# Six table chunks parted on ScalarE and TensorE, and one one-hot instruction for three pairs

## What is computed

```
emb = flat[ids + offs]
mask = (jnp.arange(L_) < lengths[..., None]).astype(emb.dtype)
pooled = jnp.einsum('bfle,bfl->bfe', emb, mask)
out = pooled.reshape(Bq, F_ * E_)
return jnp.nan_to_num(out)
```

## Time and profile before

| | |
|---|---|
| median of 3 runs | 1639.28 us |
| the profiled execution's own time | 1622.87 us |
| its span, first to last instruction | 1621.1 us |
| TensorE matmul, busy | 1003.0 us (62%) |
| VectorE, busy | 1065.0 us (66%) |
| ScalarE, busy | 509.2 us (31%) |
| GpSimd, busy | 760.1 us (47%) |
| mean granted TensorE clock | 0.792 of 2.4 GHz |
| DMA | 121.48 MB, mean 75 GB/s |

### The profile page before, as it was taken

One profiled execution on the slowest core, in us unless ns is written; L12 is line 12 of the kernel. 1 busy time (PEld: TensorE's weight loads), 2 busy tenths in 40 slices (PEclk: granted clock), 3 DMA queues, 4 the chain that ended last, 5 costly groups with the idle time before them and its releaser, 6 DMA issues.

```text
span 1621.1 us, 25785 instructions
## 1 busy us (share of the span) xinstructions
PE 1003.0 (62%) x8607; PEld 801.0 (49%) x8607; DVE 1065.0 (66%) x3021; ACT 509.2 (31%) x793; POOL 760.1 (47%) x706
## 2 busy tenths in 40 slices
PE   2757107692754816757588582881847538487886
PEld 0536006571643715636377360760735437276776
DVE  9938006793673916947599481891857629489894
ACT  2423004350422403324244140430423214143441
POOL 4845770537064172253666527166073442556110
PEclk9979558896786957968789685895877759689899
DMA  4312112132312213132334141231314113233120
GB/s 142 137 51 56 24 25 81 53 120 61 99 55 60 91 42 103 46 92 69 82 103 129 38 120 41 85 88 37 114 43 123 52 41 98 52 111 110 31 83 11
DMA packets 69225, 121.48 MB, mean 75 GB/s; under 512 B 33985, under 2 KB 35750, under 8 KB 69152
## 3 DMA queue, kind: packets, MB, share of 16 engines
q1 hardware_dynamic: 45936, 99.21, 19.0%
q0 software_dynamic: 22016, 20.93, 7.2%
q10 hardware_dynamic: 1200, 0.67, 0.2%
HBM read 79.67 MB, written 4.80 MB: 52 GB/s over the span
## 4 chain that ended last, share of the span: by engine, by line
DVE 44%; another core or an unknown queue 29%; PE 14%; issue 7%; DMA 2%; ACT 2%; SPq 1%; DVEq 0%; POOL 0%; POOLq 0%
DVE onehot_j L627 16%; PE sums L454 9%; DVE onehot_p L625 6%; DVE table L641 6%; DVE table L649 6%; DVE gathered L689 5%; PE pairs L444 4%; DMA table<-tables 2%; ACT counts L422 2%; DVE is_nan L659 1%; SPq L305 1%; DVE pooled L669 1%; DVE pooled L662 0%; DVEq L687 0%
## 5 line engine op out<-in xcount | busy, mean ns | idle before, releaser
L454 PE MATMUL sums<-table,counts 128*128 128x192 bf16 x7056 | 835.5, 262 | 209.3 <-issue 202.1
L422 ACT ACTIVATE counts<-pairs 128x588 int16<-128x588 f32 (+1 forms) x792 | 507.9, 653 | 1082.1 <-remote 547.1
L454 PEld LDWEIGHTS sums<-table,counts 128*128 128x128 fp8e3 x7056 | 667.0, 102 | 312.8 <-issue 258.3
L379 POOL DMA_INDIRECT rows<-tables,row_now x576 | 618.5, 1074 | 414.6 <-issue 414.6
L444 PE MATMUL pairs<-onehot_j,onehot_p 128*128 128x294 bf16 x1548 | 383.8, 315 | 390.2 <-ACT counts L422 164.4
L625 DVE TENSOR_TENSOR onehot_p<-ramp,p_of 128x256 bf16<-128x256 f16 x756 | 213.7, 283 | 435.1 <-remote 385.0
L627 DVE TENSOR_SCALAR onehot_j<-ramp,j_of,worth 128x296 bf16<-128x296 f16 x1512 | 493.6, 358 | 0.0
L444 PEld LDWEIGHTS pairs<-onehot_j,onehot_p 128*128 128x128 bf16 x1548 | 151.4, 101 | 488.5 <-issue 264.5
L389 POOL DMA_INDIRECT out_gathered<-gathered,place_now x56 | 70.2, 1254 | 394.0 <-DVE gathered L662 381.2
L641 DVE TENSOR_TENSOR table<-table 128x448 f32<-128x448 f32 (+1 forms) x180 | 144.4, 802 | 27.7 <-DMA table<-tables 27.0
L649 DVE TENSOR_TENSOR table<-table 128x448 f32<-128x448 f32 (+1 forms) x180 | 144.7, 804 | 0.0
(11 more groups left out here) (53 smaller groups left out, 49.0 us busy)
## 6 DMA issues: line engine op xcount, KB each, us to landing
table<-tables SPq DMA_DIRECT2D x126, 448.0 KB
rows<-zeros SPq DMA_DIRECT2D x56, 640.0 KB
rows<-tables,row_now POOLq DMA_INDIRECT x576
out_counted<-pooled SPq DMA_DIRECT2D x108, 21.0 KB
sorted_records<-records,rank POOLq DMA_INDIRECT x56
row_now<-sorted_records SPq DMA_DIRECT2D x56, 10.5 KB
out_gathered<-gathered,place_now POOLq DMA_INDIRECT x56
rows<-lookup_ids SPq DMA_DIRECT2D x1, 731.0 KB, 7.8
```

Of the source, the lines that this page charges most:

```text
L379: nc.gpsimd.indirect_dma_start(out=rows[:, k, l * E:(l + 1) * E], out_offset=None, in_=table_rows, in_offset=bass.IndirectOffsetOnAxis(ap= ...
L422: nc.scalar.activation(dst, src, ACT.Copy).then_inc(counts_saved, 1)
L454: last = nc.tensor.matmul(sums[h][:, k * PARTS * E:(k + 1) * PARTS * E], counts[h][:, j, :, k], parts[:, :, j, :, 1], start=(j == 0 and k ...
```

## The change

**Parting a chunk.** Chunks 0 to 5 of each table are no longer cut by VectorE. A new PSUM buffer `rest` of two banks holds one chunk, 448 numbers in each bank. ScalarE copies the fp32 chunk into it (`copy_chunk`). TensorE multiplies the first bf16 part by `minus_eye`, a matrix with -1 on the diagonal, and adds it onto `rest` (`take_away`, two matmuls of 448 columns), which leaves value minus first part. ScalarE writes that as bf16 into the place of the second part (`save_middle`), TensorE takes that away too, and ScalarE writes the third part (`save_low`). `PARTED_AT` gives the slot of a feature (0 to 41) at which each chunk begins: 9, 13, 17, 21, 25, 29. The three ScalarE instructions stand behind the `save_counts` of that slot and the next two; the two `take_away` stand behind the products of the next slot and the one after. A new chunk's copy waits until `rest` is read (`low_saved`). Chunk 6 stays with VectorE, in stage 12 as before.

**PSUM.** The two banks come from `pairs`, which has two buffers instead of three (`SETS = 2`).

**One-hots of p.** The three `onehot_p` instructions of a chunk become one of 128x768, ahead of the chunk's first `onehot_j`. It waits until the last pair of the chunk two stages earlier has been used.

**Start.** VectorE makes `minus_eye` once, and TensorE writes all 512 columns of both banks of `rest` once (`begin_rest`).

```diff
-SETS = 3
+SETS = 2
...
-CUTS = {3: (0, 0, 1), 4: (1, 0, 1), 5: (2, 0, 2), 6: (2, 1, 2), 7: (3, 0, 2), 8: (3, 1, 2), 9: (4, 0, 1),
-        10: (5, 0, 2), 11: (5, 1, 2), 12: (6, 0, 1)}
+PARTED_AT = {0: 9, 1: 13, 2: 17, 3: 21, 4: 25, 5: 29}
+
+PARTED_BY_VECTOR = {12: 6}
...
+        rest = psum("rest", [P, 2, 512], F32)
...
+            def copy_chunk(f, c):
+                if f == 0 and c == min(PARTED_AT):
+                    act.wait_ge(rest_begun, 1)
+                elif parted(f, c) > 1:
+                    act.wait_ge(low_saved, parted(f, c) - 1)
+                act.wait_ge(table_in[c], f * 16 + 16)
+                nc.scalar.activation(rest[:, :, 0:CE // 2], both_halves(0, c), ACT.Copy).then_inc(chunk_copied, 1)
+
+            def save_middle(f, c):
+                act.wait_ge(rest_ready, parted(f, c))
+                nc.scalar.activation(upper_of_both(1, c), rest[:, :, 0:CE // 2], ACT.Copy).then_inc(middle_ready, 1)
+
+            def save_low(f, c):
+                act.wait_ge(low_ready, parted(f, c))
+                nc.scalar.activation(upper_of_both(2, c), rest[:, :, 0:CE // 2], ACT.Copy).then_inc(low_saved, 1)
...
+                            u = slot(h, c, q)
+                            if u - 2 in begun_in:
+                                save_low(f, begun_in[u - 2])
+                            if u - 1 in begun_in:
+                                save_middle(f, begun_in[u - 1])
+                            if u in begun_in:
+                                copy_chunk(f, begun_in[u])
...
+            def begin_rest():
+
+                pe.wait_ge(eye_ready, 1)
+                pe.wait_ge(ramps_in, 32)
+                for x in range(2):
+                    last = nc.tensor.matmul(rest[:, x, :], minus_eye[:], ramp[:, 0:512], start=True, stop=True)
+                last.then_inc(rest_begun, 1)
+
+            def take_away(part, c, done):
+                for x, half in enumerate(halves_of(c)):
+                    last = nc.tensor.matmul(rest[:, x, 0:CE // 2], minus_eye[:], upper_halves(part)[:, half],
+                                            start=False, stop=True, skip_group_check=True)
+                last.then_inc(done, 1)
+
+            def part_table(f, u):
+
+                if u - 2 in begun_in:
+                    pe.wait_ge(middle_ready, parted(f, begun_in[u - 2]))
+                    take_away(1, begun_in[u - 2], low_ready)
+                if u - 1 in begun_in:
+                    pe.wait_ge(chunk_copied, parted(f, begun_in[u - 1]))
+                    take_away(0, begun_in[u - 1], rest_ready)
...
+                                if c in PARTED_AT:
+                                    pe.wait_ge(low_saved, parted(f, c))
+                                else:
+                                    pe.wait_ge(parts_ready, f * (CHUNKS - PARTED) + by_vector.index(c) + 1)
                                 pe.sem_inc(products_begun, 1)
                             multiply(1 - h, c * JC + q * JC // PAIRS, c * JC + (q + 1) * JC // PAIRS)
+                        if with_counts:
+                            part_table(f, slot(h, c, q))
...
+            def negate_eye():
+                dve.wait_ge(ramps_in, 32)
+                nc.vector.tensor_scalar(minus_eye[:], ramp_twice[:, :, 0], lane[:], -1.0, ALU.is_equal,
+                                        ALU.mult).then_inc(eye_ready, 1)
...
-                if i % 2 == 0:
+                if i == 0:
                     stage = f * STAGES + h * CHUNKS + c
                     if stage >= AHEAD:
-                        dve.wait_ge(counted, eviction_at(stage - AHEAD, i // 2) + 1)
-                    g = lookup_group(c, i)
-                    nc.vector.tensor_tensor(onehot_p[:, s, 1 + i // 2, :, :], ramp_twice,
-                                            p_of[:, 2 * f + h, g:g + 2].unsqueeze(1).to_broadcast([P, P, 2]), ALU.is_equal)
+                        dve.wait_ge(counted, eviction_at(stage - AHEAD, PAIRS - 1) + 1)
+                    of_chunk = p_of[:, 2 * f + h, c * PER_CHUNK:(c + 1) * PER_CHUNK].rearrange("p (k x) -> p k x", x=2)
+                    nc.vector.tensor_tensor(onehot_p[:, s, 1:, :, :], ramp_twice.unsqueeze(1).to_broadcast([P, PAIRS, P, 2]),
+                                            of_chunk.unsqueeze(2).to_broadcast([P, PAIRS, P, 2]), ALU.is_equal)
...
-            def cut_rest(f, c, part, parts):
-
-                sl = slice(c * CE + part * CE // parts, c * CE + (part + 1) * CE // parts)
-                if part == 0:
-
-                    dve.wait_ge(table_in[c], f * 16 + 16)
+            def cut_rest(f, c):
+
+                sl = slice(c * CE, (c + 1) * CE)
+                dve.wait_ge(table_in[c], f * 16 + 16)
...
-                    if stage in CUTS and i == 1:
-                        cut_rest(f, *CUTS[stage])
-                    if stage in CUTS and i == 4:
-                        cut_low(f, *CUTS[stage])
+                    if stage in PARTED_BY_VECTOR and i == 1:
+                        cut_rest(f, PARTED_BY_VECTOR[stage])
+                    if stage in PARTED_BY_VECTOR and i == 4:
+                        cut_low(f, PARTED_BY_VECTOR[stage])
```

40 lines of the change are left out of this document (30 added, 10 removed).

## The result

The changed kernel takes 1814.76 us (median of 4 runs, 1813.99 to 1818.2) against 1639.22 (4 runs, 1623.92 to 1640.66): a ratio of 1.1098 (1.1031 to 1.1166), 11% slower. The forecast was 1541.

What follows compares the result with a forecast made beforehand. The prediction took VectorE as the bound outside frozen stretches, where GpSimd gathers and other engines nearly stand still. 1621.1 us less 118 plus 20 frozen gave a span of 1523; 18.2 more for the median gave 1541, range 1440 to 1640.

Steps and rivals of the forecast that it cites:

- The frozen time: Stretches where GpSimd gathers and other engines nearly stand still: 578 us carried over unchanged, plus 20 us.
- the second rival: Gathers outside the frozen stretches freeze too, with VectorE idler: 236 us added, 1757 us in all; chance 0.14.
- The pass: One feature's pass outside the frozen stretches: 51.7 us, set by TensorE, instead of 59.
- TensorE's own work: TensorE's work in one pass: 44.1 us at full clock, 0.2 for two singles, 4.6 for 24 added matmuls.
- The waits: TensorE's waits in a pass: 0.4 us for the `single` to be emptied, 2.4 at the twelve `take_away`.
- 118 us: Time gained outside the frozen stretches, start and end: 7.3 us in each of 16.2 passes.
- 16.2 passes: The 954 us outside frozen stretches, start and end, counted in passes of 59 us.
- third rival: ScalarE and its hand-offs become the bound: 0.54 us at each `take_away`, pass 55.8 us, 1587 us; chance 0.14.
- VectorE's pass: VectorE's work in one feature without the removed cuts and with merged `onehot_p`: 44.6 us, down from 59.
- the table's arrival: Loading of table chunks, which ScalarE now reads: claimed to cost nothing.
- the coarser wait: One `onehot_p` per chunk waits for the last pair two chunks back: claimed covered by slack, nothing counted.
- The fourth rival: The long `onehot_p` costs 1.04 ns a number, no cheaper than three: VectorE's pass 50.2 us, 1562 us; chance 0.06.

Runs made afterwards that it cites:

- e10: The kernel before with every VectorE table cut shortened to 8 columns, still three `pairs` buffers, on a late-signal chip: 1644.9 us, ratio 1.0138 to the kernel before.
- e13: The changed kernel with GpSimd writing 128x64 integers and waiting for them behind each gather, on a late-signal chip: 1555.2 us, ratio 0.9508 to the kernel before.
- e15: The changed kernel itself, unedited, run on the same late-signal chip as e13: 1817.0 us, ratio 1.1102 to the kernel before.
- e5: The changed kernel itself on a prompt chip (no signal over 0.5 us late): 1025.4 us against 1095.3 for the kernel before, ratio 0.9364.
- e6: The changed kernel with three `onehot_p` a chunk again instead of one, on a prompt chip: 1026.4 us, ratio 0.9371 to the kernel before.
- e8: The changed kernel with second `take_away` and `save_low` one slot later and partings up to five slots apart, on a late-signal chip: 1783.9 us against 1599.4 before.
- e11: The changed kernel with one more register load from SBUF behind each gather, on a late-signal chip: 1744.6 us, ratio 1.073 to the kernel before.
- e9: The kernel before with two `pairs` buffers instead of three, on a late-signal chip: 1642.0 us against 1620.9 for the kernel before.

## Why the prediction was wrong

**The step that failed is "The frozen time".** It took the frozen time as fixed because GpSimd's work is, and added 20 us; it grew by 226 (131 to 182 by close variants of the rule), as the second rival has it with 236 (chance 0.14). The term was read from busy shares, where the sum looked like a property of the gathers. It was not one: it hangs on what the other engines do meanwhile. The cuts, which the change removes, had been slowing the gathers, and the copies, which it adds, stand between the late signals. The earlier trace rows showed the first: a gather had a mean of 1074 ns while the one in the earlier trace rows takes 1.00. The rival had "an idler VectorE" as its reason. e10 confirms that VectorE's missing cuts suffice for two thirds of it, the lateness; the last third, ScalarE's 66 us, is in no rival. That pausing GpSimd after each gather cures it is shown by e13 against e15. That the cuts protect through the gathers' density, and not also by keeping the pipeline behind, rests on the timeline and the table and has no run of its own. That 226 lies so near 236 is in part luck: the rival lets all 181 spared gathers freeze, and 102 more did (489 against 387).

**The pass.** 51.7 us was forecast. It is 53.9 on a prompt chip (e5) and 55.3 in the last feature of the result. TensorE's own work was right, 49.05 against 48.9. The waits were 4.9 instead of 2.8 (ahead of `take_away` 2.96 for 2.4, the rest 1.9 for 0.4): the two writes from `rest` take 1.18 us, not the 0.92 that the price of an eviction gave; the copy into PSUM takes 0.928 as forecast. The wait ahead of a `take_away` for L467 is 0.23 us on average (25.0 over 107), the forecast 0.2, but longer ones lie under the weight loads. Why the last pass of the result is 1.4 us longer than e5's is open.

**Where 118 us went.** Outside the frozen stretches 34 us were gained. A pass 3.7 us shorter gives 60 over 16.2 passes. The other 26 were not taken apart, and with another rule for the stretches the 34 are less or nothing. Restarts are a part: there are 28 stretches instead of 18, and after one, at the lower clock (0.50 from 334 to 355 us, which is 1.2 GHz), ten products take 1.81 us (352.30) against 1.02. The sum: 1541 + 206 more frozen + 84 less gained - 16, since the median lies 2.6 us above the profiled span and not 18, gives 1815. One sum of the prediction is off by itself: its third rival leaves out the 20 us of frozen time that the forecast adds, and comes to 1607 us instead of 1587.

**Right.** `onehot_p` at 557 ns (forecast 550), so 0.52 ns a number holds; VectorE's pass 44.96 (44.6); 36 cuts of 1085 ns; the table's arrival and the coarser wait cost nothing that shows (e6 equals e5). The fourth rival is out. Where nothing freezes the direction was right and the size too large: 70 us gained, not 118.

The rule that the prediction took from the Trainium skill, "SBUF — State Buffer", section Who interferes with whom, that TensorE never waits on anyone there, is not refuted by the changed kernel: TensorE's matmuls ran at pace (ten products in 1.02 us at 330.11), and its signals were late. In the kernel before, products stood 2.5 us with no wait that the profile names; whether that bears on the rule is open.

## What to carry to other kernels

When a stretch stands still, find the first instruction that waits for something already recorded as done; that tells a late signal from a stopped engine. Look at both kernels: here the one before had both. Before taking work off an engine, ask which other engine it had been slowing and whether something depended on that slowness: here 257 us less on VectorE, with denser indirect DMAs, went with a kernel 11% slower on a late chip. A change can have opposite signs on two chips, so time the kernel before beside every run.

## What the runs showed of the hardware

- TensorE's semaphore signals can arrive late, by up to 33 us, while GpSimd issues indirect DMAs 1.30 us apart, in the result and in e8 to e11 and e15, but not on the prompt chips. One follows the other: ScalarE stood 9.85 and then 9.95 us in the timeline. With 2.1 us between gathers, and a wait after each, one is late (e13). The changed kernel's signals to TensorE were not late.
- In the same stretches, with three `pairs` buffers, TensorE's products can start 1.4 to 3.5 us apart with nothing to wait for: 202 us of such idle time before, 356 in e10, none in e9 with two buffers.
- The traces of those chips also hold fewer records of semaphore updates, 10336 for the changed kernel against 20561 for the same file in e5, and 15603 in e13, where few signals are late. Most of the missing ones are of landing DMAs (6193 against 16022 in e5), the others are 4143 against 4539. Whether the recording itself is what makes signals late wasn't tried.
- ScalarE reads 128x896 fp32 from PSUM and writes bf16 into every second 16-bit place in 1.18 us; from SBUF into PSUM as fp32 in 0.93. Which side costs the 0.25 us wasn't separated.
- A register load between two indirect DMAs does not space them (e11, 1.30 us in the median); an instruction whose write is waited for does (e13, 2.10).
- Beside an fp32 `tensor_tensor` cut of VectorE an indirect DMA takes 1.5 to 1.9 us on GpSimd; the mean of 576 gathers is 1074 ns with the cuts and 1005 without.
